# Constant matmuls on TensorE at five stage borders of a fused two-layer transformer kernel

## The chip, the cores and the metric

The kernel runs on one NeuronCore of one Trainium2 chip. The metric is the device time of one launch in microseconds (us). Five engines work side by side and meet through semaphores: TensorE (PE; its weight loads are listed apart as PEld), VectorE (DVE), ScalarE (ACT), GpSimd (POOL) and SyncE (SP), which here only issues DMAs. TensorE has two clock levels, 1.2 and 2.4 GHz; the profile gives the granted share of the higher one (0.50 or 1.00, or a mean between them over a stretch).

## The reference, cut to what matters

Two transformer layers on x of 4 x 1024 tokens x 128 channels, all in f32:

```python
x = x + attn0(layernorm(x))    # 16 heads of 8 channels, relative position bias with a gate
x = x + ffn0(layernorm(x))     # 16 experts of 64, grouped top-k routing, one shared expert
x = x + attn1(layernorm(x))    # 8 heads, q and k of 64 channels, values of 128, summed over heads
x = x + ffn1(layernorm(x))     # FP4-quantised linear layers, 352 hidden channels
```

The routing sorts per token: `scores = sigmoid(x @ w_gate.T)`, the two best of four groups by the sum of their two best scores, and of their experts the four best, whose scores are divided by their sum.

## The kernel before, in words

The program is a list of stages, each a block of its own: weights, `phase_project0`, `phase_attend0`, `phase_output0`, `phase_route`, `phase_experts`, `phase_project1`, `phase_attend1`, `phase_quant_ffn`. At the end of each block every engine drains its own work and meets the others at a barrier (the rows of L434, L1169, L1290, L1415, L1577 in the trace); so the engine that finishes last, SP's waits for stores included, sets when the next block begins. Within a block each engine has its own instruction stream, in the order in which the code is written, and TensorE runs its matmuls strictly in that order.

`phase_project0` works on 8 chunks of 512 tokens: layer norm, transposes, q, k, v and gates; its last act is that SP stores q and k to DRAM and waits until they have landed. `phase_attend0` has 64 items (16 heads x 4 batches) of 8 tiles of 128 queries. Row maxima are computed `LEAD` = 12 tiles ahead of the exponentials: TensorE writes a score tile of 128x1024 into two of three ring banks (L853 the far part, L867 the diagonal band), DVE reduces each 128x512 half to its maximum (L1048), and the bank is free again. So the stage opens with 12 tiles of maxima alone (the lead), then comes for each tile the score product for the exponential (L889, L899), ACT's exp (L1032) and the product with the values (L947). After 8 tiles the maxima of the first item are turned on TensorE (L964), go by ACT and SP into the operand of the exp product, and the first exp product waits for that DMA.

`phase_output0` is a software pipeline over the 8 chunks, written by `pipeline(eng, stages)`: at step s a stage with lag k works on chunk s - k, and the stages are issued in the order of the list. On TensorE that is the output projection (L1227, lag 2), the transpose of the normalised x (L1234, lag 4), the transpose of the attention output (L1220, lag 1) and the routing product (L1241, lag 5). DVE adds the bias (L1253), adds to x (L1256), takes the statistics and normalises (L364); POOL copies the attention output (L1177) and takes the reciprocal root; ACT moves transposed data out of PSUM.

`phase_route` ranks the experts on DVE alone. TensorE waits for the result (`ready`), turns it in 8 groups of four 128x128 transposes (L1368), and ACT copies each group out (L1375).

`phase_project1` makes q and k of the second attention (three f16 products L382 to L384 for each output of 128x512) and again ends when its stores have landed. `phase_attend1` has 32 items and the same lead of 12 tiles of maxima: two matmuls of 512 columns per tile (L1826), each reduced by DVE (L1949). In the steady state it is two matmuls per exp product (L1836, L1837) and three per value product (L1848 to L1850).

Before its first matmul in a block TensorE runs `credit` (L63), semaphore increments that come one after the other.

Of the kernel before, what the change touches and what calls it, by code (L numbers as in the profile page):

```python
# [368 lines left out]
def steps(eng, body, total=NC):  # L369


    with eng.Fori(0, total // 2 - 1) as i:
        body(2 * i, 0, False)
        body(2 * i + 1, 1, False)
    body(total - 2, 0, False)
    body(total - 1, 1, True)


def product16(nc, out, w, x):


    nc.tensor.matmul(out, w[:, 0, :], x[0], start=True, stop=False)  # L382
    nc.tensor.matmul(out, w[:, 0, :], x[1], start=False, stop=False)
    return nc.tensor.matmul(out, w[:, 1, :], x[0], start=False, stop=True)  # L384
# [7 lines left out]
def phase_project0(nc, g, a):  # L392
# [4 lines left out]
    with ExitStack() as ctx:  # L397
# [36 lines left out]
        with nc.Block() as block:  # L434
# [67 lines left out]
            def _(pe):  # L502
# [31 lines left out]
                    nc.tensor.matmul(ps[:, GR, 0:CT * H0], g.flip[:, :], gate[:, u, :, :], start=True, stop=True).then_inc(s.gate_turned, 1)  # L534

                steps(pe, step)

            @block.vector
            def _(dve):
# [110 lines left out]
def phase_attend0(nc, g, a):  # L650
# [9 lines left out]
    with ExitStack() as ctx:  # L660
# [22 lines left out]
        EXP, RING, AV = 0, 4, 7  # L683
# [55 lines left out]
        with nc.Block() as block:  # L739
# [87 lines left out]
            def _(pe):  # L827
# [132 lines left out]
                def turn_m(h, b, at):  # L960
# [3 lines left out]
                    nc.tensor.matmul(ps[0:2 * TB, RING + at % BANKS, 0:P], mm[:, b % 2, :, :, :].rearrange("p x y t -> p (x y t)"), ident16[:, :],  # L964
                                     start=True, stop=True).then_inc(s.m_turned, 1)

                for t in range(LEAD):
                    if t % TB == 0:
                        wait_loaded(0, t // TB)
                    at = [lead.index((t, half)) for half in range(2)]  # L970
                    for x in at:
                        if x >= BANKS:
                            if lead[x - BANKS] == "m":
                                pe.wait_ge(s.m_moved, done(0))
                            else:
                                pe.wait_ge(s.max_read, done(2 * lead[x - BANKS][0] + lead[x - BANKS][1]))
                    maxima(t // TB, t % TB, [RING + (x + shift) % BANKS for x in at])
                    if t == TB - 1:
                        at = lead.index("m")
                        pe.wait_ge(s.max_read, done(2 * lead[at - BANKS][0] + lead[at - BANKS][1]))  # L980
                        turn_m(0, 0, FIRST_M)
# [135 lines left out]
def pipeline(eng, stages, total=NC):  # L1117

    lag = max(k for k, _ in stages)
    pairs = (total - lag) // 2

    def straight(s):
        for k, stage in stages:
            if 0 <= s - k < total:
                stage(s - k, (s - k) % 2)

    for s in range(lag):
        straight(s)  # L1130
    with eng.Fori(0, pairs) as i:
        for r in range(lag, lag + 2):
            for k, stage in stages:
                stage(2 * i + (r - k), (r - k) % 2)
    for s in range(lag + 2 * pairs, total + lag):
        straight(s)


def phase_output0(nc, g, a):

    with ExitStack() as ctx:
# [27 lines left out]
        with nc.Block() as block:  # L1169
# [43 lines left out]
            def _(pe):  # L1213
# [27 lines left out]
                        last = nc.tensor.matmul(ps[:, R, k * NE:(k + 1) * NE], xTs[:, u, k * P:(k + 1) * P], g.routeW[:, :], start=True, stop=True)  # L1241
                    last.then_inc(s.r_psum, 1)

                pipeline(pe, [(2, project), (4, turn_x), (1, turn_a), (5, route)])

            @block.vector
            def _(dve):
# [19 lines left out]
def phase_route(nc, g, a):  # L1267


    with ExitStack() as ctx:  # L1270
# [19 lines left out]
        with nc.Block() as block:  # L1290
# [71 lines left out]

            @block.tensor
            def _(pe):
                pe.wait_ge(ready, 1)
                for c in range(NC):
                    for k in range(CT):
                        ins = nc.tensor.transpose(ps[0:2 * NE, c, k * P:(k + 1) * P], parts[:, c * CT + k, :], g.ident[:, :])  # L1368
                    ins.then_inc(turned, 1)
# [177 lines left out]
def phase_project1(nc, g, a):  # L1547

    with ExitStack() as ctx:
# [27 lines left out]
        with nc.Block() as block:  # L1577
# [56 lines left out]
            def _(pe):  # L1634
# [23 lines left out]
                        product16(nc, ps[:, QK + i % RING, :], g.w16[:, :, IN_16[W_Q1 + i], :], x).then_inc(s.qk_psum, 1)  # L1658

                pipeline(pe, [(2, lambda n, u: project(n, u, FIRST)), (1, turn_x), (2, lambda n, u: project(n, u, REST))])  # L1660

            @block.vector
            def _(dve):
# [25 lines left out]
def phase_attend1(nc, g, a):  # L1689
# [5 lines left out]
    with ExitStack() as ctx:  # L1695
# [19 lines left out]
        EXP, MAX, AV, OUT = 0, 2, 4, 6  # L1715
# [37 lines left out]
        with nc.Block() as block:  # L1753
# [57 lines left out]
            def _(pe):  # L1811
# [40 lines left out]
                def project_y(h, b, k, last_item=False):  # L1852
# [14 lines left out]
                        last = nc.tensor.matmul(out, y[0], w[1], start=False, stop=True)  # L1867
                    last.then_inc(s.out_psum[k], 1)

                for t in range(LEAD):  # L1870
                    score_max(0, t // TB, t % TB)
                    if t == TB - 1:
                        turn_m(0, 0)
# [404 lines left out]
```

## Time and profile before

| | us |
|---|---|
| median of 3 runs (lowest, highest) | 2301.78 (2299.64, 2307.66) |
| the profiled execution | 2315.67 |
| its span, first to last instruction | 2313.9 |
| TensorE busy | 2010.6 (87%) |
| VectorE busy | 1630.1 (70%) |
| ScalarE busy | 1347.9 (58%) |
| GpSimd busy | 1091.8 (47%) |
| mean granted TensorE clock | 0.943 |

The profiled execution took 13.9 us more than the median of the runs, and 1.8 us of its time lie outside of the span. Times in the trace count from the span's start. TensorE's busy time contains the latency at the end of each matmul, so the distance between the starts of two matmuls that follow each other closely, not the duration of one, is what a matmul costs.

### The profile page before, as it was taken

How to read it: one execution, taken by the hardware profiler on the slowest of the kernel's cores; microseconds unless marked ns; L12 is line 12 of the kernel's file. 1: busy time of each engine (PE TensorE's matmuls, PEld its weight loads, DVE VectorE, ACT ScalarE, POOL GpSimd, SP SyncE). 2: the span in 40 equal slices, each digit the busy share in tenths (PEclk: the TensorE clock that was granted, in tenths of full speed). 3: DMA queues.
4: the chain of work that ended last, by engine and by line, in shares of the span. 5: the costliest groups of instructions: out<-in, count | busy, mean ns of one | idle time of the engine just before them, and what ended most of it. 6: DMA issues, size and time to landing. Idle time of an engine off the chain costs nothing. (4 is left out here: it accounts for less than half of the span.)

```text
span 2313.9 us, 56417 instructions
## 1 busy us (share of the span) xinstructions
PE 2010.6 (87%) x17787; PEld 1018.8 (44%) x17787; DVE 1630.1 (70%) x3441; ACT 1347.9 (58%) x2150; POOL 1091.8 (47%) x939
## 2 busy tenths in 40 slices
PE   5569999999999989875799759999999999997666
PEld 3324444444444444434344214444444444443444
DVE  4778888888888877767666776666666666664696
ACT  2226666666666655552455437777777777776221
POOL 1132322322232222324355317777877787777454
PEclk9869999999999999986899979999999999999797
DMA  5522211221122121100000460011111011100000
GB/s 132 154 62 53 55 51 48 55 54 49 51 55 51 48 55 46 48 11 1 1 1 0 144 201 29 29 42 28 41 28 42 28 42 28 42 14 1 0 19 19
DMA packets 127068, 107.33 MB, mean 46 GB/s; under 512 B 39636, under 2 KB 102724, under 8 KB 126956
## 3 DMA queue, kind: packets, MB, share of 16 engines
q1 hardware_dynamic: 124640, 103.37, 16.3%
q10 hardware_dynamic: 2316, 2.64, 0.4%
q8 instruction: 49, 0.80, 0.1%
q14 instruction: 63, 0.52, 0.1%
HBM read 76.01 MB, written 29.53 MB: 46 GB/s over the span
## 5 line engine op out<-in xcount | busy, mean ns | idle before, releaser
L1048 DVE TENSOR_REDUCE b_mx<-psum 128x1 f32<-128x512 f32 x1024 | 663.5, 686 | 160.2 <-PE psum L867 92.9
L1032 ACT ACTIVATE b_prob<-psum 128x1024 f32<-128x1024 f32 x512 | 523.9, 1023 | 334.1 <-PE psum L899 334.0
L1806 POOL TENSOR_TENSOR f_plo<-f_prob,f_phi 128x512 f16<-128x512 f32 x512 | 586.8, 1156 | 170.2 <-ACT f_phi L1931 145.2
L1949 DVE TENSOR_REDUCE f_mx<-psum 128x1 f32<-128x512 f32 x512 | 328.4, 682 | 169.5 <-PE psum L1826 168.4
L1930 ACT ACTIVATE f_prob<-psum 128x512 f32<-128x512 f32 x512 | 308.1, 602 | 158.3 <-PE psum L1837 153.5
L947 PE MATMUL psum<-b_prob,b_v 128*32 128x256 f32 x4096 | 330.3, 394 | 1.6 <-ACT b_prob L1032 0.5
L1931 ACT ACTIVATE f_phi<-psum 128x512 f16<-128x512 f32 x512 | 306.9, 599 | 0.0
L805 POOL COPY b_v<-v 128x64 f32 x64 | 15.1, 236 | 610.2 <-PE psum L947 609.8
L899 PE MATMUL psum<-b_diag,b_toep 128*128 128x79 f16 (+1 forms) x4224 | 269.2, 209 | 0.0
L899 PEld LDWEIGHTS psum<-b_diag,b_toep 128*128 128x128 f16 x4224 | 237.5, 99 | 9.4 <-issue 2.6
L808 POOL TENSOR_TENSOR b_diag<-flip,grev 128x1024 f16<-128x1024 f16 x128 | 239.6, 1892 | 0.0
L1836 PE MATMUL psum<-f_qa,f_ka 128*128 128x512 f16 x512 | 195.2, 381 | 10.4 <-ACT f_phi L1931 7.2
L1848 PE MATMUL psum<-f_phi,v 128*128 128x512 f16 x512 | 194.3, 380 | 1.0 <-DVE f_yT L1968 0.5
L1837 PE MATMUL psum<-f_qb,f_kb 128*128 128x512 f16 x512 | 194.8, 380 | 0.0
L1849 PE MATMUL psum<-f_phi,v 128*128 128x512 f16 x512 | 194.0, 379 | 0.0
L1850 PE MATMUL psum<-f_plo,v 128*128 128x512 f16 x512 | 194.0, 379 | 0.0
L1826 PE MATMUL psum<-f_ka,f_qa 128*128 128x512 f16 x512 | 165.4, 392 | 19.0 <-DMA f_kb<-d_qk 13.2
L867 PE MATMUL psum<-b_toep,b_diag 128*128 128x286 f16 (+2 forms) x640 | 150.4, 269 | 0.0
L1512 POOL TENSOR_TENSOR d_h<-d_hid,d_h 128x512 f16<-128x512 f32 x72 | 83.2, 1157 | 110.8 <-ACT d_h L1482 110.8
L1968 DVE SCALAR_TENSOR_TENSOR f_yT<-psum,f_yT 128x512 f16<-128x512 f32 x64 | 44.2, 691 | 94.6 <-ACT f_yT L1917 94.6
L867 PEld LDWEIGHTS psum<-b_toep,b_diag 128*128 128x128 f16 x640 | 51.4, 97 | 115.3 <-issue 115.3
L947 PEld LDWEIGHTS psum<-b_prob,b_v 128*32 128x32 f32 x4096 | 81.2, 108 | 44.3 <-ACT b_prob L1032 1.0
(312 smaller groups left out, 3407.9 us busy)
## 6 DMA issues: line engine op xcount, KB each, us to landing
d_qk<-e_qk SPq DMA_DIRECT2D x64, 256.0 KB, 2.6
b_toep<-d_line SPq DMA_DIRECT2D x128, 64.0 KB
f_qa<-d_qk SPq DMA_DIRECT2D x64, 128.0 KB, 2.8
f_ka<-d_qk SPq DMA_DIRECT2D x64, 128.0 KB, 2.9
b_q<-d_q SPq DMA_DIRECT2D x128, 54.0 KB
d_k<-a_qk SPq DMA_DIRECT2D x48, 128.0 KB, 2.3
b_toep<-d_line SPq DMA_DIRECT2D x128, 32.0 KB
b_q<-b_m SPq DMA_DIRECT2D x256, 1.0 KB
```

What stands on the lines that cost most here:

```text
L808: ins = nc.gpsimd.tensor_tensor(diag[:, b, part, :, :], g.flip16[:, :].rearrange("p (a n) -> p a n", a=1).to_broadcast([P, TB, P]), gates. ...
L867: return nc.tensor.matmul(ps[:, bank, n0 - c0:n1 - c0], diag[:, b, 0, t, :], toep[:, b, 0, u:u + n1 - n0], start=False, stop=True, skip_gr ...
L899: last = nc.tensor.matmul(ps[:, bank, at + x:at + y], toep[:, b, tp, blk * P:(blk + 1) * P], diag[:, b, dp, qt, x:y], start=False, stop=(t ...
L947: last = nc.tensor.matmul(ps[32 * c:32 * c + VW, AV, 0:2 * P], vs[:, b, t, :], prob[:, t % 4, c * 2 * P:(c + 1) * 2 * P], start=t == 0, st ...
L1032: nc.scalar.activation(prob[:, t % 4, :].rearrange("p (a n) -> p a n", a=2), ps[:, EXP + 2 * (t % 2):EXP + 2 * (t % 2) + 2, :], ACT.Exp).t ...
L1048: nc.vector.tensor_reduce(mx[:, b, t, half:half + 1], ps[:, bank, :], AX.X, ALU.max).then_inc(s.max_read, 1)
L1806: nc.gpsimd.tensor_tensor(plo[:, t % 4, at], prob[:, t % 4, at], phi[:, t % 4, at], ALU.subtract).then_inc(s.plo_ready, 1)
L1836: nc.tensor.matmul(ps[:, EXP + half, :], ka[b][:, keys], qa[b][:, queries], start=True, stop=False)
L1837: nc.tensor.matmul(ps[:, EXP + half, :], kb[b][:, keys], qb[b][:, queries], start=False, stop=True).then_inc(s.exp_psum, 1)
L1930: nc.scalar.activation(prob[:, t % 4, at], ps[:, EXP + half, :], ACT.Exp)
L1931: nc.scalar.activation(phi[:, t % 4, at], ps[:, EXP + half, :], ACT.Exp).then_inc(s.exp_ready, 1)
L1949: nc.vector.tensor_reduce(mx[:, b, t, half:half + 1], ps[:, MAX + half, :], AX.X, ALU.max).then_inc(s.max_read, 1)
```

## The change

A helper `keep_busy` issues `count` matmuls of a constant f16 128x128 (`flip16`) with a constant f16 128x512 (`expert`) into a PSUM bank whose content nobody reads any more or yet. Nothing waits for them and they wait for nothing, but they stand in TensorE's stream, which is in order, and in its drain at the end of a block. The numbers are 48 at the end of `phase_project0` and 48 at the start of `phase_attend0`, 20 at the start of `phase_output0` and 6 at the end of each of 8 of its steps, 110 at the start of `phase_route`, 40 at the end of `phase_project1` and 40 at the start of `phase_attend1`. These are the whole diff.

```diff
+def keep_busy(nc, g, bank, count):
+
+    for _ in range(count):
+        nc.tensor.matmul(g.ps[:, bank, :], g.flip16[:, :], g.expert[:, 0:4, :].rearrange("p f e -> p (f e)"), start=True, stop=True)
...
                 steps(pe, step)
+                keep_busy(nc, g, 1, 48)
...
+                keep_busy(nc, g, AV, 48)
                 for t in range(LEAD):
                     if t % TB == 0:
                         wait_loaded(0, t // TB)
...
-                pipeline(pe, [(2, project), (4, turn_x), (1, turn_a), (5, route)])
+                keep_busy(nc, g, 7, 20)
+                pipeline(pe, [(2, project), (4, turn_x), (1, turn_a), (5, route), (1, lambda n, u: keep_busy(nc, g, 7, 6))])
...
             def _(pe):
+                keep_busy(nc, g, 0, 110)
                 pe.wait_ge(ready, 1)
                 for c in range(NC):
...
                 pipeline(pe, [(2, lambda n, u: project(n, u, FIRST)), (1, turn_x), (2, lambda n, u: project(n, u, REST))])
+                keep_busy(nc, g, 6, 40)
...
+                keep_busy(nc, g, AV, 40)
                 for t in range(LEAD):
                     score_max(0, t // TB, t % TB)
```

TensorE's stream at the start of `phase_output0` before: the transpose of the attention output (`c_at`), the output projection (`c_aT`), the transpose of the normalised x (`c_xn`). The line numbers after the change are higher by 8 here.

```order
L1212 UNCONDITIONAL_BRANCH
L1220 MATMUL psum<-square,c_at 128x128 x4
L1227 MATMUL psum<-wT,c_aT 128x128 x4
L1220 MATMUL psum<-square,c_at 128x128 x4
L1227 MATMUL psum<-wT,c_aT 128x128 x4
L1220 MATMUL psum<-square,c_at 128x128 x4
L1227 MATMUL psum<-wT,c_aT 128x128 x4
L1234 MATMUL psum<-square,c_xn 128x128 x4
```

And the same place now, with the constant matmuls as `expert,flip`:

```order
L1220 UNCONDITIONAL_BRANCH
L382 MATMUL psum<-expert,flip 128x512 x20
L1228 MATMUL psum<-square,c_at 128x128 x4
L382 MATMUL psum<-expert,flip 128x512 x6
L1235 MATMUL psum<-wT,c_aT 128x128 x4
L1228 MATMUL psum<-square,c_at 128x128 x4
L382 MATMUL psum<-expert,flip 128x512 x6
L1235 MATMUL psum<-wT,c_aT 128x128 x4
L1228 MATMUL psum<-square,c_at 128x128 x4
```

The 20 stand ahead of the first real work of the stage, and the 6 stand between the last product of a step and the projection that opens the next one.

TensorE's stream from the end of `phase_project1` (f16 products of `x` and `w`) into `phase_attend1` (score products of `f_ka` and `f_qa` for the maxima), now:

```order
L390 MATMUL psum<-x,w 128x512
L382 MATMUL psum<-expert,flip 128x512 x40
L1587 UNCONDITIONAL_BRANCH
L1821 UNCONDITIONAL_BRANCH
L382 MATMUL psum<-expert,flip 128x512 x40
L1837 MATMUL psum<-f_ka,f_qa 128x512 x16
L1829 MATMUL psum<-square,f_negm 8x128
```

Before, the two branches with the barrier between them followed the last product directly, and the first score product followed the branches. From `phase_project0` into `phase_attend0` it is the same with 48 and 48.

## Rows read from the trace of the kernel before

**Rows 1.** The page, busy tenths in 40 slices: TensorE's granted clock

```profile
PEclk9869999999999999986899979999999999999797
```

**Rows 2.** Windows: busy us of PE, PEld, DVE, ACT, POOL, granted clock, DMA share, GB/s

```profile
100.00:105.00 5.00, 0.00 (x0) 0.00 (x0) 3.94 (x9) 0.00 (x0) 0.00 (x0) 0.68 0.70 202
...
125.00:130.00 5.00, 2.82 (x12) 0.69 (x12) 2.80 (x5) 0.00 (x0) 5.00 (x5) 0.50 0.38 104
...
150.00:155.00 5.00, 5.00 (x62) 2.52 (x59) 2.97 (x6) 2.38 (x3) 0.00 (x0) 0.70 0.00 0
...
1070.00:1075.00 5.00, 3.09 (x25) 2.78 (x25) 4.84 (x21) 1.85 (x5) 2.94 (x4) 0.96 0.01 3
...
1115.00:1120.00 5.00, 4.89 (x27) 3.35 (x25) 0.00 (x0) 3.60 (x8) 0.00 (x0) 0.60 0.00 0
```

**Rows 3.** Timeline (start, us, engine, line, idle before), f16 matmuls early in phase_experts

```profile
1121.87 0.38 PE L384 MATMUL psum<-x,w 128*128 128x512 f16 x1
...
1122.09 0.38 PE L382 MATMUL psum<-x,w 128*128 128x512 f16 x1
```

**Rows 4.** Timeline, end of phase_project1 and start of phase_attend1

```profile
1355.44 0.63 PE L383 MATMUL psum<-x,w 128*128 128x512 f16 x1
...
1355.86 0.63 PE L384 MATMUL psum<-x,w 128*128 128x512 f16 x1
...
1360.11 0.38 PE L384 MATMUL psum<-x,w 128*128 128x512 f16 x1
...
1373.67 1.03 PE L1826 MATMUL psum<-f_ka,f_qa 128*128 128x512 f16 x2 [13.18 <-DMA f_kb<-d_qk]
...
1374.32 11.04 DVE L1949 TENSOR_REDUCE f_mx<-psum 128x1 f32<-128x512 f32 x16 [4.64 <-PE psum L1826]
```

**Rows 5.** TensorE's credits after the barriers of three blocks: count, ns, first and last

```profile
L63 PEldq EVENT_SEMAPHORE  x7: 51/51/51, 1366.6 to 1367.6; - x7
...
L63 PEldq EVENT_SEMAPHORE  x6: 51/51/51, 114.1 to 114.9; - x6
...
L63 PEldq EVENT_SEMAPHORE  x4: 51/51/51, 1037.8 to 1038.2; - x4
```

**Rows 6.** Timeline, end of phase_project0 and first tiles of phase_attend0

```profile
97.40 0.33 PE L534 MATMUL psum<-a_gate,square 128*128 128x64 f32 x2
...
125.26 0.28 PE L853 MATMUL psum<-b_k0l,b_q 32*128 32x128 f16 x1 [27.53 <-DMA b_toep<-d_line]
...
129.78 1.29 DVE L1048 TENSOR_REDUCE b_mx<-psum 128x1 f32<-128x512 f32 x2 [0.55 <-PE psum L867]
...
146.61 0.61 PE L889 MATMUL psum<-b_q,b_k0l 32*128 32x512 f16 x2 [0.20 <-DMA b_q<-b_m]
...
153.19 1.02 ACT L1032 ACTIVATE b_prob<-psum 128x1024 f32<-128x1024 f32 x1 [1.57 <-PE psum L899]
...
154.67 1.02 ACT L1032 ACTIVATE b_prob<-psum 128x1024 f32<-128x1024 f32 x1 [0.46 <-PE psum L899]
```

**Rows 7.** Timeline, phase_output0

```profile
1038.69 1.12 PE L1220 MATMUL psum<-square,c_at 128*128 128x128 f32 x4 [9.57 <-POOL c_at L1177]
...
1042.59 0.69 DVE L1253 TENSOR_TENSOR c_o<-psum,bvo 128x512 f32<-128x512 f32 x1 [5.18 <-PE psum L1227]
...
1051.27 0.69 DVE L1253 TENSOR_TENSOR c_o<-psum,bvo 128x512 f32<-128x512 f32 x1 [1.93 <-PE psum L1227]
...
1068.16 0.66 PE L1234 MATMUL psum<-square,c_xn 128*128 128x128 f32 x4 [0.35 <-DVE c_xn L364]
...
1070.47 1.16 PE L1227 MATMUL psum<-wT,c_aT 128*128 128x128 f32 x8
...
1071.83 0.68 DVE L1253 TENSOR_TENSOR c_o<-psum,bvo 128x512 f32<-128x512 f32 x1
```

**Rows 8.** Timeline, phase_route

```profile
1113.65 6.24 PE L1368 MATMUL psum<-square,r_parts 128*32 128x128 f32 x32 [29.96 <-DVE r_parts L1355]
...
1114.73 0.57 ACT L1375 CAST combT<-psum 32x512 f16<-32x512 f32 x1 [30.78 <-PE psum L1368]
```

## The prediction

> **What bounds the kernel now.** I read first the line of the granted clock over the whole span [rows 1]. The reader is to see that it is at 2.4 GHz (9, in tenths) almost everywhere: the dips lie at slices 2 and 3, 18 to 20 and 24, and near the end. All that a warmer TensorE could give lies there. Then I went through the dips in stretches of 5 us [rows 2], and through the timeline at each border [rows 4, 6 to 8], asking two questions: what does TensorE wait for there, and is it TensorE at all that sets the pace once it works?
>
> The answer differs from place to place. In the gap between the projection and the first attention (97.7 to 125.3) TensorE waits for DMAs: the first product comes after 27.53 us idle, released by a load [rows 6]. In the 12 tiles of maxima that follow, a DVE pair of 1.29 us sets most of the pace, and DVE waits 0.55 us for a slow product in the tile shown [rows 6]. In the output projection DVE is busy 4.84 of 5 us [rows 2]. In the routing TensorE waits 29.96 us for DVE's ranks, and then turns 32 tiles in 6.24 us at the low clock [rows 8]. Before the second attention it waits 13.18 us for stores, barrier and loads, and then DVE's 16 reductions take 11.04 us, 0.69 each, with nothing between them [rows 4]: that stretch cannot get faster by the clock.
>
> **The price of one constant matmul.** Products of the same form, an f16 weight of 128x128 and 512 columns, start 0.22 us apart at 2.4 GHz (1121.87 and 1122.09) [rows 3], and 0.42 us apart at 1.2 GHz (1355.44 and 1355.86) [rows 4]. From 512 columns I take 0.215 and 0.427. So n of them cost 0.215 n, plus half of the time that passes before the clock rises. How long is that? In the routing the turns began at 1113.65 and the slice 1115 to 1120 has a mean clock of 0.60, so it rose at about 1119.0: 5.3 us [rows 2, 8]. In the first attention close work began at 146.61, and a mean of 0.70 in 150 to 155 puts the rise at 153.0: 6.4 us [rows 2, 6]. I take 5.3, which adds 2.6 us, and as bounds 2.7 us (half of it, no row shows less) and 6.4 us, which add 1.3 and 3.2.
>
> **Start of the first attention.** The 48 at the end of the projection begin at 97.7 at full clock, end at 108.1 and are over before SP's stores let the barrier pass near 114: nothing. But the clock does not survive what follows. After the last work at 97.73 it fell within 100 to 105 (mean 0.68, so at 101.8) [rows 2, 6], 4.1 us later, and from 108.1 to the next constants there are 6.8 us. These wait for TensorE's own credits, of which the last is at 114.9 [rows 5]. They end at 114.95 + 48 x 0.215 + 2.6 = 127.9, and the first real product waited only until 125.26: **2.6 us later** (1.3 to 3.3). What is queued behind is the whole lead, and DVE waits for it. In return the first two or three tiles of the lead run at 2.4 GHz and save DVE some 0.4 each of its 0.55, say 1.0. The first exp product waited 0.20 us for the DMA of the maxima at 146.61, which now is there: another 0.3 with the issue before it. Sum **+1.3**. I do not count on the clock holding through the lead: there TensorE was busy 2.82 of 5 us at the low clock, about half of that at the high one, and in 1070 to 1075 the clock fell with 3.09 of 5 us busy [rows 2].
>
> **The output projection.** TensorE's credits end at 1038.25 [rows 5], and the first turn stood ready at 1038.69 [rows 7]. The 20 constants begin with the clock low and end at 1038.25 + 4.3 + 2.6 = 1045.2: **+6.5** (5.2 to 7.1). Nothing covers that: POOL's copy is done, and ACT, DVE and the rest of the chain start from this turn. At the high clock the way from the first turn to DVE's first sum (1038.69 to 1042.59, 3.90 us) becomes 0.43 + 6 constants of 1.29 + a projection of 1.16, about 3.0, and from there to the third sum (1051.27) it loses some 0.7 as well: -1.6 [rows 7]. Then each step holds 6 constants. From a turn of x at 1068.16 to the end of the next projection (1070.47 + 1.16) it was 3.47 us; with 1.29 more it is 4.76. DVE's own step is about 3.8 us: 3.67 from this turn, which DVE's last instruction released, to its next sum at 1071.83, and the time to wake. The turn waits for DVE's step, and DVE's step after the next waits for that projection, so two steps take 4.76 + 0.05 + 3.8 = 8.6, or 4.3 each. The five steps from 1051.27 to 1071.83 took 4.11 each, the cold ones included, so the five lose 0.95. The tail has no constants between its turns and stays as it is. Sum 6.5 - 1.6 + 0.95 = **+5.9**. So the constants inside the loop about pay for themselves, the 20 ahead of it do not.
>
> **The routing.** The 110 take 23.7 + 2.6 = 26.3 us of the gap of 29.96, and nothing waits for them. They end about 3.2 us before the ranks are ready. If the clock holds, the 8 groups are paced by ACT's 0.57 instead of 0.78 (6.24 / 8): 8 x 0.21 = 1.7 us less [rows 8]. A pause of 3.2 us is near the 4.1 us above, so I count half: **-0.8** (0 to -1.7).
>
> **The second projection and attention.** The last product starts at 1360.11 and the constants at 1360.33 [rows 4]; 40 x 0.215 = 8.6 puts TensorE's drain at about 1369.1. The barrier was open at 1366.55, as the first credit at 1366.6 shows [rows 5]: everything in the next block, SP's loads too, is **2.8 us** later. The credits, which took until 1367.65, then end at 1370.45. The clock is still up. 40 more end at 1379.1, and the first score product was at 1373.67; its load now lands at 1376.5 and no longer decides. The lead starts **5.45 us** later in all, the 2.8 included. DVE's pace there is its own [rows 4], so a high clock returns 0.3, at the first wait and at the turn of the maxima: **+5.1**. Once the exp products begin the stage is bound by TensorE for 700 us, so no slack takes this back.
>
> **Sum.** 1.3 + 5.9 - 0.8 + 5.1 = 11.5 us. The profiled execution, 2315.67, would become 2327; it was 13.9 above the median of the runs, for which the forecast is 2301.78 + 11.5 = **2313.3 us**. About 0.3% (6.9 us) is what a measurement of this kernel can tell from no change.
>
> **One rule against the rows.** Rows 3 say 0.215 us for a constant. The Trainium skill, in TensorE: Matmul & The Clock Gate, section Back-to-back issue gap, gives for a sustained stream of weight loads and matmuls of 512 columns about 131 ns each. This case's trace disagrees, with its 0.22 us between two such starts [rows 3]. By the page 40 constants would take 5.2 us instead of 8.6, the sum of the second attention would be near nothing, and the whole change, by an estimate from that page, near +4 us.
>
> **The rivals.**
> 1. *The constants are cheaper than rows 3 say, because they need nobody's result* (0.06). The point at which it decides is the second projection: at or under 0.15 us each, 40 fit into the 6 us between 1360.33 and the barrier and into the 6.0 us between credits and load, and the 5.1 goes. For it speaks nothing in the rows but that products of 32 rows start together in other places; against it [rows 3]. Time: 11.5 - 5.1 - 1.3 - 1 = +4, 2306. The page's figure above would have this outcome.
> 2. *The clock holds through both leads into the exp products* (0.17), which is the way to "not slower". Its place is 128 to 150. Then DVE loses its waits in all tiles of the lead (another 1.5 us), and the first exps come 1.1 us earlier each (idle 1.57 at 153.19, 0.46 at 154.67) [rows 6], some 2.0 in all; the routing gives its full 1.7, and the second attention's first exps 0.6. That is -3.5 - 0.9 - 0.6: **+6.5**, 2308.3. It decides when the granted clock is 1.00 from 128 to 153. Against it stands the fall at 3.09 of 5 us busy.
> 3. *Constants do not raise the clock* (0.05), since they are mostly zeros. Then 48, 20, 110 and 40 cost 0.427 each: 20.5 us against 10.3 at the first attention, 8.5 ahead of the output projection and 2.6 in each of its steps (some 20 us), 47 against 30 in the routing, 17 against 6 twice: about +70, 2372.
> 4. *The stages do not start from TensorE's stream as I read it, or steady stages settle in another rhythm* (0.07), either sign, 2295 to 2325.
>
> The forecast itself has 0.65.
>
> **How the numbers follow.** Within the likeliest case the bounds of the clock's rise (-2.6 to +1.2 over both places), the routing (-0.9 to +0.8) and the repeat of a median of 2301.78 (some 3 us) give 2308 to 2319. Reaching to rivals 1 and 2 on one side, and on the other to a clock that rises late and to an experts stage that begins cold, makes 2303 to 2322, which leaves out rival 3 and most of 4. Slower by over 0.3% means above 2308.7: nearly all of the forecast, less than half of rival 2, rival 3, part of 4, together 0.68. Faster than 2294.9 is left to rival 4 and to what I overlook: 0.08. The rest, 0.24, is the same.
>
> **What would show each step.** In the profile of the changed kernel: constants 0.215 us apart, at 0.427 for 2.7 to 6.4 us after each cold start; the first product of the first attention at 126.6 to 128.6, released by TensorE's own stream and no longer by a DMA; clock 0.50 again before 140; the first turn of the output projection some 6.5 us after the credits, and steps of 4.3 us; the ranks ready after the constants end; the drain of the second projection ending last on TensorE, and the first score product 9.8 us after its barrier and not 7.1. The prediction would be wrong if the lead of the first attention ran at 1.00 throughout and its tiles came 0.3 us apart closer, if the constants stood closer than 0.2 us, or if the 20 turned out to begin before the barrier.

## The result, and the profile after

The changed kernel took 2313.33 us (median; 2309.67 to 2317.40), beside 2301.22 us for the kernel before on the same chip: a ratio of 1.0046, 95% interval 1.003 to 1.0062. It is slower by 12 us by this comparison, and the fastest single runs lie 10 us apart too (2309.67 and 2299.64). The profiled execution took 2314.96 us, its span is 2313.2 us and its mean clock 0.959. That is no longer than the profiled execution of before (2315.67 us), and this section and the next show why both numbers hold.

The clock over the 40 slices, as in [rows 1]:

```profile
PEclk8979999999999999988999999999999999999797
```

The dips at slices 20 and 24 are gone, slice 19 rises from 6 to 8, and slices 2 and 3 rise by one tenth each (8 and 6 before, 9 and 7 now). The windows show where the clock came up and where it did not stay (columns as in [rows 2]):

```profile
125.00:130.00 5.00, 4.32 (x22) 1.74 (x20) 0.65 (x2) 0.00 (x0) 5.00 (x5) 1.00 0.39 106
130.00:135.00 5.00, 2.55 (x12) 0.71 (x12) 3.85 (x8) 0.00 (x0) 1.67 (x1) 0.64 0.45 121
...
150.00:155.00 5.00, 5.00 (x43) 2.35 (x43) 3.08 (x6) 2.05 (x2) 0.00 (x0) 0.50 0.01 3
...
1110.00:1115.00 5.00, 4.41 (x25) 3.29 (x26) 0.54 (x1) 2.64 (x5) 0.00 (x0) 0.66 0.00 0
```

In 125 to 130 the clock is at its high level where it was at 0.50; in 130 to 135 it falls, after two tiles of the lead, and at 150 it is as low as it ever was. Now the start of the first attention, to be laid beside [rows 6] (start, us, engine, line, idle before):

```profile
97.00 10.52 PE L382 MATMUL psum<-expert,flip 128*128 128x512 f16 x48
115.46 13.34 PE L382 MATMUL psum<-expert,flip 128*128 128x512 f16 x48 [7.93 <-PEq L440]
128.73 0.23 PE L860 MATMUL psum<-b_k0l,b_q 32*128 32x128 f16 x1
...
151.46 1.02 ACT L1040 ACTIVATE b_prob<-psum 128x1024 f32<-128x1024 f32 x1 [7.15 <-PE psum L906]
```

The same 48 matmuls take 10.52 us warm and 13.34 us when the clock starts low, and the first real product comes behind them with no DMA named. The first exp starts at 151.46. In the kernel before it was this row, with a barrier 0.45 us earlier:

```profile
148.73 1.02 ACT L1032 ACTIVATE b_prob<-psum 128x1024 f32<-128x1024 f32 x1 [7.25 <-PE psum L899]
```

The output projection, beside [rows 7]:

```profile
1027.41 7.00 PE L382 MATMUL psum<-expert,flip 128*128 128x512 f16 x20 [9.22 <-PEq L746]
...
1034.25 0.60 PE L1228 MATMUL psum<-square,c_at 128*128 128x128 f32 x4
...
1037.31 1.46 PE L382 MATMUL psum<-expert,flip 128*128 128x512 f16 x6
...
1041.80 0.66 PE L1228 MATMUL psum<-square,c_at 128*128 128x128 f32 x4 [2.14 <-POOL c_at L1185]
1042.29 2.26 PE L382 MATMUL psum<-expert,flip 128*128 128x512 f16 x6
...
1044.34 1.92 PE L1235 MATMUL psum<-wT,c_aT 128*128 128x128 f32 x8
...
1046.30 0.69 DVE L1262 TENSOR_TENSOR c_o<-psum,bvo 128x512 f32<-128x512 f32 x1 [2.53 <-PE psum L1235]
...
1064.00 0.69 DVE L1262 TENSOR_TENSOR c_o<-psum,bvo 128x512 f32<-128x512 f32 x1 [0.87 <-PE psum L1235]
...
1067.98 0.68 DVE L1262 TENSOR_TENSOR c_o<-psum,bvo 128x512 f32<-128x512 f32 x1
```

The first turn waits for the 20. Each later group of 6 takes 1.46 us, but the one after TensorE's wait for POOL (2.14 us) takes 2.26, and the projection behind it 1.92 instead of 1.16: the clock fell just behind that wait. DVE's last two sums are 3.98 us apart, the two before them 4.77: it waits for TensorE in every second step.

The second projection and attention, beside [rows 4]; the first row is one of the barrier's (duration three times, first and last start):

```profile
L1587 PEldq DRAIN  x1: 4050/4050/4050, 1362.3 to 1362.3; - x1
...
1367.69 8.79 PE L382 MATMUL psum<-expert,flip 128*128 128x512 f16 x40 [1.36 <-issue]
1376.32 0.59 PE L1837 MATMUL psum<-f_ka,f_qa 128*128 128x512 f16 x2
...
1376.73 10.45 DVE L1961 TENSOR_REDUCE f_mx<-psum 128x1 f32<-128x512 f32 x16 [7.03 <-PE psum L1837]
```

TensorE's drain ends at 1366.35 and releases the barrier at 1366.5, where SP was ready at 1363.8. The first score product comes 9.8 us after it. DVE's 16 reductions take 10.45 us instead of 11.04.

**Length of each block.** The whole time of this kernel scatters by several us for a reason shown below, so the experiments are read by blocks. A block's length is the time from TensorE's release at one barrier to that at the next, as in these rows of the changed kernel, 1026.5 - 114.4 = 912.1 us for the first attention (such rows are rounded to 0.1 us, and so are the lengths):

```profile
L440 PEldq EVENT_SEMAPHORE  x1: 51/51/51, 114.4 to 114.4; - x1
...
L746 PEldq EVENT_SEMAPHORE  x1: 51/51/51, 1026.5 to 1026.5; - x1
```

| block | without constants (profiles) | changed kernel, profiled twice | difference |
|---|---|---|---|
| first projection | 76.95 (6: 76.9 to 77.0) | 77.9, 78.4 | +1.2 |
| first attention | 909.0 (2 free of stalls), 914.8 to 923.6 (6 others) | 912.1, 911.8 | +2.9 against 909.0 |
| output projection | 46.4 (10: 45.4 to 48.1) | 54.5, 53.7 | +7.7 |
| routing | 36.5 (9: 35.8 to 36.9) | 35.9, 34.3 | -1.4 |
| experts | 163.9 | 163.8, 163.9 | 0 |
| second projection | 82.3 (10: 81.2 to 83.4) | 85.8, 85.1 | +3.2 |
| second attention | 766.9 (10: 766.3 to 767.4) | 767.6, 769.3 | +1.6 |

The sum is +15.2 us. Two blocks are not in the table, since no constants stand in them: the weights (35.1 to 37.5 us) and the last one, `phase_quant_ffn` (178.7 to 181.1 us). They differ by over 2 us from profile to profile with their instructions unchanged. In the first pair of profiles the last block alone gives the changed kernel 2.1 us.

The kernel before pays part of that in another way: its first attention in the profile is 923.6 us long, since it holds two stalls (engine, line, idle before):

```profile
867.29 0.61 PE L889 MATMUL psum<-b_q,b_k1l 32*128 32x512 f16 x2 [3.74 <-issue]
...
869.13 1.02 ACT L1032 ACTIVATE b_prob<-psum 128x1024 f32<-128x1024 f32 x1 [5.10 <-PE psum L899]
...
928.37 0.61 PE L889 MATMUL psum<-b_q,b_k1l 32*128 32x512 f16 x2 [4.57 <-issue]
```

"issue" means that TensorE waited for nothing that the profile shows. Both places are the first work behind the back edge of the attention's loop (the jump back to its first instruction), 61.1 us apart, which is one pass. The changed kernel has no such wait.

### The profile page after: what moved, and what is told of

Same layout as the page of the kernel before. It is cut to its first block and busy times, and to the rows that moved or that the text cites. A ratio compares the mean times of both kernels' runs of the same rounds, so it can differ in the third digit from the quotient of the medians.

```text
span 2313.2 us, 57125 instructions
## 1 busy us (share of the span) xinstructions
PE 2075.1 (90%) x18141; PEld 1045.6 (45%) x18141; DVE 1632.1 (71%) x3441; ACT 1347.0 (58%) x2150; POOL 1091.4 (47%) x939
## 5 line engine op out<-in xcount | busy, mean ns | idle before, releaser
L1056 DVE TENSOR_REDUCE b_mx<-psum 128x1 f32<-128x512 f32 x1024 | 663.9, 686 | 148.5 <-PE psum L874 85.1
L382 PE MATMUL psum<-expert,flip 128*128 128x512 f16 x354 | 86.1, 404 | 19.1 <-PEq L746 9.2
```

What stands on the lines that cost most here:

```text
L1056: nc.vector.tensor_reduce(mx[:, b, t, half:half + 1], ps[:, bank, :], AX.X, ALU.max).then_inc(s.max_read, 1)
```

## The experiments

### One place at a time

The first four kernels each keep the constants of one place. The second attention:

```diff
+                keep_busy(nc, g, 6, 40)    # end of phase_project1
+                keep_busy(nc, g, AV, 40)   # start of phase_attend1
```

> Only the 40 constants at the end of the second projection and the 40 at the start of the second attention. My theory (a constant costs 0.215 us in TensorE's in-order stream, and what it exceeds its gap by is lost): barrier 2.8 us later, first score product 9.8 us after the barrier and not 7.1, +5.1 us in all, ratio 1.0022. Rival (the loss of the whole change comes from other places, such as instruction fetch or the output projection): within 1 us of before, and the first score product still released by its load.

Measured: second projection 85.2 us, second attention 767.9, first score product 9.78 us after its barrier: the same as in the changed kernel. The whole: 2315.19 us, ratio 1.003 (0.9996 to 1.0064). These two blocks cost +2.9 and +1.0 by this profile. The lead starts 2.4 us later than without constants (7.2 to 7.5 us after the barrier), but the sixth exp only 1.0 later (32.9 us after the barrier against 31.5 to 32.1): the warm clock returns over 1 us in the lead.

The 20 ahead of the output projection:

```diff
+                keep_busy(nc, g, 7, 20)
```

> Only the 20 constants ahead of the output projection. My theory: its first turn comes 7.4 to 8 us after the barrier and not 1.1, +6.5 us, of which the steps return less than 1 since without the six per step the clock falls again: block of 52 us and not 46.5, ratio 1.0025. Rival (a warm start pays the wait back): block of 47 to 49 us.

Measured: block 50.1 us, +3.7 against 46.4; whole 2304.81 us, ratio 0.9997 (0.9973 to 1.0021). The first turn is 7.9 us behind the barrier instead of 1.1; from it to DVE's third sum it takes 10.34 us instead of 12.6, and from the third to the eighth 19.45. Without constants that last stretch takes 19.5 us in five of ten profiles, where the clock holds, and 20.6 to 22.1 in the others, where it falls once more on the way. So the 20 give back 2.2 us in the fill, and 1.0 in the loop against the mean of 20.5, and pay 6.8 for it. The block lies between the two readings, 52 and 47 to 49.

The two places around the first attention:

```diff
+                keep_busy(nc, g, 1, 48)    # end of phase_project0
+                keep_busy(nc, g, AV, 48)   # start of phase_attend0
```

> Only the 48 at the end of the first projection and the 48 at the start of the first attention. My theory: first product some 3 us later than before, the clock falls again within the lead, sum +1.3 us (0 to 2.5), ratio 1.0006. Rival (the clock at the start is worth its wait): -2 us or less.

Measured: first projection 78.4 us, first attention 911.7 and no stall, first exp 36.8 us after the barrier; whole 2304.03 us, ratio 0.9973 (0.9951 to 0.9995).

The 110 ahead of the routing's turns:

```diff
+                keep_busy(nc, g, 0, 110)
```

> Only the 110 constants in the routing. My theory: they cover 26 of 30 us and then the clock falls or holds by chance, routing block 34.9 to 36.6 us and not 36.6, -0.8 us on average, ratio 0.9997. Rival (the clock surely holds): -1.7 us, block of 34.9 with a granted clock of 1.00 through the turns.

Measured: routing 35.8 us; whole 2307.83 us, ratio 1.0012 (0.9986 to 1.0038). The clock did not hold through the turns, though the constants end only 2.70 us before them (the window 1105 to 1110 has 0.73):

```profile
1107.06 5.34 PE L1375 MATMUL psum<-square,r_parts 128*32 128x128 f32 x32 [2.70 <-DVE r_parts L1361]
```

Two kernels without the 110 had 35.8 and 35.9 us (the one above, and the one with the 6 per step below), so a single profile doesn't decide this term.

The kernel with the first attention's constants should have been 1 to 3 us slower than before and came out faster. Its block had no stall, those of the other three had 1, 2 and 1. So the question became whether this is chance.

### The kernel before again, and the 6 per step alone

> The kernel before, unchanged, to see how much of a difference its own executions make. In the four experiments so far the first attention without any constants was 914.8, 916.7, 922.7 and (kernel before) 923.6 us long, and held 1, 1, 2 and 2 stalls of TensorE of 4 to 5 us just behind its loop's back edge. If these stalls are chance in each execution, this one may hold any number from 0 to 2. If they belong to the program's code as placed, it holds 2 again and the block is near 923 us. Either way the other blocks should repeat within 1 us: projection 77, output projection 45 to 48, routing 36.5, second projection 82 to 83, second attention 767. Ratio 1.000.

Measured: 2306.64 us, ratio to itself 1.0028 (1.0001 to 1.0055); first attention 915.8 us with one stall; all other blocks within 1.2 us of the first profile. So two groups of runs of one and the same kernel differ by 0.3%, with an interval that leaves out 1: here a ratio within 0.3% of 1 says little by itself. And the number of stalls changes from one execution of the same kernel to the next.

```diff
-                pipeline(pe, [(2, project), (4, turn_x), (1, turn_a), (5, route)])
+                pipeline(pe, [(2, project), (4, turn_x), (1, turn_a), (5, route), (1, lambda n, u: keep_busy(nc, g, 7, 6))])
```

> Only the 6 constants at the end of each step of the output projection. Against four blocks without constants there (45.4, 46.6, 48.1, 48.1 us, mean 47.05) the prediction's step says about nothing: the steady steps grow from 4.11 to 4.3 us, and the fill gives 1.6 us back. The blocks with the 20 alone (50.1) and with both (54.5) say instead that the 6 per step cost 4.4 us. If they do so by themselves, this block is 50 to 52 us long and its steps alternate between 3.9 and 4.8 us; if it was only the pair, or a pause that happened to let the clock fall in the changed kernel, it is 46 to 48. The rest as in the kernel before; the whole time +0 to +4 us, which the timed runs can hardly tell.

Measured: block 48.0 us, below the 50 to 52 of one reading and at the upper edge of the other, +1.6 against the mean of 46.4, which is within the scatter of 45.4 to 48.1; whole 2308.48 us, ratio 1.0019 (0.9995 to 1.0042). Its timeline shows the alternation:

```profile
1061.65 1.05 PE L1233 MATMUL psum<-wT,c_aT 128*128 128x128 f32 x8
...
1062.74 0.69 DVE L1259 TENSOR_TENSOR c_o<-psum,bvo 128x512 f32<-128x512 f32 x1 [0.87 <-PE psum L1233]
...
1066.71 0.68 DVE L1259 TENSOR_TENSOR c_o<-psum,bvo 128x512 f32<-128x512 f32 x1
```

From the third sum to the eighth it takes 21.70 us, in the changed kernel 21.68 and 21.70. The 20 alone cost 3.7 and the 6 alone 1.6, both together 7.7, which is 2.4 more than the sum. With the 6 behind them the 20 no longer bring the short loop (21.7 us instead of 19.45), because now TensorE and no longer DVE sets every second step; and of the 2.2 us in the fill 0.6 are left.

### Counts cut to the gaps

```diff
+                keep_busy(nc, g, 1, 48)    # end of phase_project0, as in the change
+                keep_busy(nc, g, AV, 36)   # start of phase_attend0, was 48
+                keep_busy(nc, g, 0, 122)   # phase_route, was 110; none in phase_output0
+                keep_busy(nc, g, 6, 26)    # end of phase_project1, was 40
+                keep_busy(nc, g, AV, 27)   # start of phase_attend1, was 40
```

> The same constants cut to what the waits of the profile can hold: 48 at the end of the first projection, 36 ahead of the first attention, none in the output projection, 122 ahead of the routing's turns, 26 at the end of the second projection, 27 ahead of the second attention. If a constant matmul costs only its own 0.215 us in TensorE's stream (theory), then: first product of the first attention as early as in the kernel before plus at most 0.3 us, the lead a little faster; output projection 47; routing 35.5; barrier after the second projection as before (82.5); first maximum product of the second attention 7.2 to 7.4 us after its barrier as before and the block 766.5. Sum -1 to -2.5 us against blocks free of stalls, and with the stalls of the first attention gone as in the changed kernel, 2300 to 2303 us in all, ratio 0.996 to 0.999. Rival: constants cost something beyond their time in the stream (the drain, the barrier, a colder start of what follows), then the second projection and attention stay 1 us or more longer although nothing waits for TensorE, and the whole is at or above the kernel before.

Measured: first attention 908.3 us, output projection 48.1, routing 34.3, second projection 83.2, second attention 766.4; whole 2300.59 us, ratio 0.9979 (0.996 to 0.9998). The 27 still put the first score product at 8.4 us after the barrier instead of 7.3, but the sixth exp comes at 31.4 us, no later than without constants. The rival's extra cost beyond the time in the stream is not to be seen: 83.2 is within the scatter of 81.2 to 83.4.

### What the constants do to the place of the code

```diff
+                keep_busy(nc, g, 1, 48)    # end of phase_project0, alone
```

> Only the 48 at the end of the first projection, which lie in the wait for its stores: 77 to 78 us for that block by both theories. What it is for is the first attention, whose instructions are unchanged but lie 48 matmuls further on in TensorE's code. In the profiles so far that block held 2 stalls of 4 to 5 us behind the loop's back edge in two kernels without constants ahead of it, 1 in two others, and 0 in both kernels with constants ahead of it (911.7 and 912.1 us, 2.4 of them from the late start). Theory one, placement: moving the code is enough, the stalls are gone, the block takes 909 to 911 us, and the timed runs lie within 5 us of each other as those of the two kernels without stalls did. Theory two, the warm clock or the constants at the start of the attention remove them: here the clock has fallen again before the attention starts, so the block holds 1 or 2 stalls, 914 to 923 us. Theory three, chance: any number.

Measured: first attention 909.0 us, no stall; 2299.14 us, all runs within 7.4 us of each other, ratio 0.9979 (0.9965 to 0.9993). The clock was low again when the attention began (0.50 from 115 to 150). So it is placement, or TensorE's work, but not the clock. The next kernel has no work:

```diff
+                for _ in range(96):
+                    pe.sem_inc(g.x_loaded, 1)
```

> No constant matmul at all: in the place of the 48 (each a weight load and a matmul) at the end of the first projection stand 96 increments of a semaphore that nobody waits for, some 5 us of TensorE's queue inside the wait for the stores, and the same number of instructions ahead of the first attention's loop. Theory one, placement: the stalls of 4 to 5 us behind the loop's back edge are gone, the first attention takes 909 to 910 us, the runs lie within 8 us of each other and the median is 2298 to 2300. Theory two, TensorE's work or clock: the block holds 1 or 2 stalls, 914 to 923 us, and the runs spread over 15 us or more. By theory one SP's late store in the first projection (1.2 to 1.8 us instead of 0.33, in all four kernels with the 48) tells more: if it is gone here (block 77.0), the matmuls' traffic caused it; if it stays (78.3), the code did.

Measured: first attention 909.0 us, no stall; 2300.27 us, ratio 0.9972 (0.9953 to 0.9992). The increments run in TensorE's queue from 96.5 to 111.2, inside the wait for stores. So 96 instructions without any matmul remove the stalls as 48 constants do. And with a third as many instructions:

```diff
+                keep_busy(nc, g, 1, 16)    # end of phase_project0, alone
```

> 16 constants instead of 48 at the end of the first projection, so that the loop of the first attention is moved by 32 instructions instead of 96. If any move removes the stalls: 0 stalls, 909 us. If what counts is where exactly the loop's instructions come to lie: 1 stall or 2 may be left, 914 to 918 us. If it is chance (the kernel before itself had 2 and 1): any number, and runs spread over 15 us or more.

Measured: **2406.73 us, ratio 1.0434 (1.0398 to 1.047)**. None of the expectations had that. All blocks but one are as ever; the first attention takes 1014.3 us, 105.3 more than 909.0, and holds 14 stalls, 61 us apart, one for each pass of the loop from the second on. One of them in its timeline, the load of the first score product behind the back edge:

```profile
217.44 0.10 PEld L896 LDWEIGHTS psum<-b_q,b_k1l 32*128 32x128 f16 x2 [3.35 <-issue]
...
218.76 1.02 ACT L1039 ACTIVATE b_prob<-psum 128x1024 f32<-128x1024 f32 x1 [3.69 <-PE psum L906]
...
220.63 0.19 PEld L954 LDWEIGHTS psum<-b_prob,b_v 128*32 128x32 f32 x5 [1.92 <-issue]
```

Two waits stand here with "issue", 3.35 and 1.92 us, and behind them the clock is low for a stretch (window of the same kernel):

```profile
220.00:225.00 5.00, 4.37 (x36) 1.66 (x37) 1.36 (x3) 1.40 (x2) 3.12 (x3) 0.50 0.29 43
```

The group of that weight load, in this kernel and then in the one with 96 increments (busy and mean ns, then idle before it in us):

```profile
L896 PEld LDWEIGHTS psum<-b_q,b_k1l 32*128 32x128 f16 x192 | 12.9, 96 | 50.3 <-issue 50.3
```

```profile
L897 PEld LDWEIGHTS psum<-b_q,b_k1l 32*128 32x128 f16 x192 | 12.3, 92 | 6.6 <-issue 6.6
```

The page's row of the queue that carries instructions points to what TensorE waits for. In the kernel before, with the 16 constants, with the 96 increments, and in the changed kernel:

```profile
q8 instruction: 49, 0.80, 0.1%
```

```profile
q8 instruction: 157, 2.57, 0.4%
```

```profile
q8 instruction: 32, 0.52, 0.1%
```

```profile
q8 instruction: 34, 0.56, 0.1%
```

The first two numbers are packets and MB. It is 8 to 9 packets of 16 KB more for each stall, over all profiles of the study:

| instructions ahead of the loop, more than before | kernels | stalls | q8 packets | first attention, us |
|---|---|---|---|---|
| 0 | before, before again, and the four with one other place | 2, 1, 1, 2, 1, 1 | 49, 40, 41, 49, 41, 41 | 914.8 to 923.6 |
| 32 | 16 constants | 14 | 157 | 1014.3 |
| 96 | 48 constants, 96 increments | 0, 0 | 32, 32 | 909.0, 909.0 |
| 168 | 48 and 36 constants (twice) | 0, 0 | 33, 33 | 908.3, 907.8 |
| 192 | changed kernel (twice), 48 and 48 constants | 0, 0, 0 | 34, 34, 32 | 911.7 to 912.1 |

The same row for stretches of the trace says when the packets come. In the kernel before there is none from 220 to 860, and 13 from 860 to 935, which holds the two stalls. With the 16 constants they come in each pass, 112 from 215 to 980; with the 96 increments there is none from 215 to 980.

```profile
q8 instruction: 13, 0.21, 1.4%
```

```profile
q8 instruction: 112, 1.84, 1.0%
```

In the four profiles with one stall, which lies between 213 and 225, 9 packets come from 213 to 290 and none from 290 to 970. So from the second pass on the loop fetches nothing in a pass without a stall, and a stall stands where some 9 packets are fetched again.

The two kernels with 96 show that the stalls go away when 96 instructions of either kind stand ahead of the loop. The 14 stalls with 32 more instructions were not repeated with 32 increments, so there the place of the code is argued, not shown. That the stalls are fetches of instructions is read from the packets, their times and the place behind the back edge; no run here took the fetch itself away. Which offsets are good could not be told from five of them.

### The free places together, and the changed kernel again

```diff
+                keep_busy(nc, g, 1, 48)    # end of phase_project0
+                keep_busy(nc, g, AV, 36)   # start of phase_attend0
+                keep_busy(nc, g, 0, 122)   # phase_route
```

> Only the constants that the block lengths so far show to be free or better: 48 at the end of the first projection, 36 ahead of the first attention, 122 ahead of the routing's turns; nothing in the output projection or around the second attention. Theory (each place by itself): first attention 908 to 909 us and without a stall as in the kernel with the cut counts (908.3), routing 34.3 against 36.5 to 36.9, output projection 45.4 to 48.1, second projection 81 to 83, second attention 766.5; against the kernel with the 48 of the projection's end alone (2299.1 us) that is 0.7 + 2.2 = 3 us less, 2296 us, ratio 0.996 to 0.998, the upper end if the output projection loses its clock once more. Rival: what the routing gives back is taken again by the blocks behind it, as the kernel with the cut counts hinted (2300.6 us although these two blocks gave 3 us); then it is 2299 to 2301.

Measured: first attention 907.8 us, output projection 45.4, routing 34.3; 2298.98 us, ratio 0.9967 (0.9946 to 0.9988). It beats both kernels, the changed one by 14 us. The kernel with 96 idle increments, timed with it, took 2300.27 us, so of the gain over the kernel before most is the placement; 1.3 us are left to the warm clock where the profile promised 3, and that is not more than the runs scatter. The routing in this kernel's timeline:

```profile
1066.68 28.72 PE L382 MATMUL psum<-expert,flip 128*128 128x512 f16 x122 [0.57 <-PEq L1177]
...
1096.12 3.67 PE L1377 MATMUL psum<-square,r_parts 128*32 128x128 f32 x32 [0.71 <-DVE r_parts L1363]
```

The constants end 0.71 us before the ranks, and the 32 turns take 3.67 us instead of 6.24 [rows 8].

> The changed kernel itself once more, on the same chip as the other three. Blocks as in its first profile: projection 78, first attention 912 and no stall, output projection 54.5 if TensorE's clock falls in the wait for the third chunk's copy as it did (52.5 if not), routing 36, second projection 85.5, second attention 767.7; 2313 us, and 13 to 15 us above the kernel with the 48 of the projection's end alone. If the two blocks of the output projection differ by over 1 us, the term that came out too large was chance in one profile.

Measured: 2313.39 us, ratio 1.0027 (0.9999 to 1.0054) against a kernel before that took 2305.91 us this time. The changed kernel repeats to 0.1 us; it is the kernel before that moves, from 2302 to 2307 us in three groups of runs on this chip, with 2301 beside the first result and 2308 on the chip of the first four experiments. So by this second comparison of whole times alone the change could not be told from no change. Output projection 53.7 us with the same fall of the clock, so its term was no chance. The routing took 34.3 us this time, and 35.9 in the first profile. The turns in the first profile, after 110 constants, and then here:

```profile
1110.59 5.34 PE L1378 MATMUL psum<-square,r_parts 128*32 128x128 f32 x32 [4.28 <-DVE r_parts L1364]
```

```profile
1110.04 3.67 PE L1378 MATMUL psum<-square,r_parts 128*32 128x128 f32 x32 [3.79 <-DVE r_parts L1364]
```

In the first profile the clock fell right behind the wait of 4.28 us (0.66 in the window of 1110 to 1115 above), here it held behind 3.79 us. But in the kernel with the 110 alone it fell behind 2.70 us, so the length of the wait alone doesn't decide it. The 110 brought the short turns in one profile of three, the 122, which leave less than 1 us, in both of two.

## Why the prediction was right, and where not

The time, 2313.3 forecast and 2313.33 measured, was right, and the likeliest case was the one that came. But two errors of several us cancelled in it, and the agreement to 0.1 us is luck. Step by step:

- **Price of a constant.** 0.215 us: confirmed, 48 in 10.52 us. The cold start added 2.6 in the forecast; the 48 of the first attention took 13.34 us, so it added about 2.8 here. The rule of the Trainium skill (TensorE: Matmul & The Clock Gate, Back-to-back issue gap) that the prediction weighed, 131 ns, does not hold for this stream.
- **First projection, forecast 0.** Mis-sized: +1.2. TensorE's drain was over long before SP, as said, but one of SP's stores is issued late. In the kernel with the 48 alone it is this row, 1.66 us where the same store took 0.33 in the kernel before:

```profile
98.69 1.66 SPq L457 DMA_DIRECT2D d_q<-a_g  x1
```

  It is so in 5 of the 6 profiles with 48 constants there (1.2 to 1.8 us), and not in those with 16 or with increments; the block with the 96 increments took 77.6 all the same. What holds the store is open.
- **Start of the first attention, forecast +2.6 - 1.3.** Right in kind: the first product came behind the constants (at 128.73, 0.1 later than the latest time named), and the clock was at 0.50 again before 140. By the first exp, 37.0 us after the barrier against 34.4, it is +2.5, and +2.9 by the block. The first product came 3.1 us later than without constants, where 2.6 were forecast. The return of the lead was mis-sized: 1.3 were forecast and some 0.6 came, since the clock fell after two tiles.
- **Output projection, forecast +5.9, measured +7.7.** The start: +6.5 forecast, +6.6 measured. The steady steps: five of 4.3 forecast (21.5 us), 21.7 measured, alternating as said (3.98 + 4.77 = 8.75 for two, 8.6 forecast). They cost 1.1 to 1.2 against 0.95. Mis-sized is the fill: -1.6 forecast, and from the first turn to the third sum it is 12.0 us instead of 12.6, -0.6. The first sum did come 1.1 us sooner after the turn (0.9 forecast); from the first to the third it took 0.4 to 0.5 us longer, where 0.7 less was forecast. The 18 constants between the first turn and the third projection cost 1.7 (10.34 us in the kernel with the 20 alone), the fall of the clock behind TensorE's wait for POOL among them. The prediction costed the fill as if the high clock were sure after the 20. The remaining 0.3 are in the tail, 13.02 and 12.35 us against 12.3, and not explained.
- **Routing, forecast -0.8 as the mean of 0 and -1.7.** Measured -0.6 and -2.2: it is the two-sided case that was forecast, with a larger gain. The -0.6 is not the constants' doing for sure, since two kernels without them had the same length. The prediction let the length of the pause decide (3.2 us beside 4.1); the clock fell behind 2.70 us and held behind 3.79, so more than that decides.
- **Second projection, forecast +2.8.** +3.2, with TensorE's drain ending last, as said.
- **Second attention, forecast +2.3 behind its barrier.** The start at 9.8 us was exact. The return was mis-sized: 0.3 forecast, and against a start 2.4 us later the block grew by only 0.7 and 2.4 us in the two profiles and by 1.0 in the kernel with this place alone, so 0 to 1.7 came back. Part of it is that DVE's 16 reductions shrank from 11.04 to 10.45 us, a stretch of which the prediction said that it cannot get faster by the clock.
- **What the prediction left out.** The sum of the terms by blocks is +15.2 against 11.5, and the timed runs agree: from the kernel with the 48 of the projection's end alone, 2299.14 us, to the changed one it is 14.2, and 1.2 of that block are in both. The constants ahead of the first attention also move its code, and with it went the stalls that cost the kernel before 6 to 15 us in each of six profiles, and some 1 to 9 us in its timed medians (2301 to 2308 us, against 2299.14 and 2300.27 in the two kernels that only moved the code). The profile showed them: two waits of 5.10 and 5.93 us of ACT for TensorE, "issue" in front. The prediction read the stage as steady and did not ask what 192 instructions ahead of a loop do to it. Of its rivals the fourth came nearest (a steady stage in another rhythm) but named no mechanism. Rival 1 is refuted by the first row of constants (48 in 10.52 us, 0.22 each), rival 2 by the window of 130 to 135, and rival 3 by the second row: 13.34 us, where 48 at the low clock would take 20.5.

## What to carry to other kernels

A matmul that nobody reads is free only inside a wait that it does not outlast, and the clock that it buys can be gone after the next short wait of the real work (2.14 us in the output projection). Here it paid in the routing, where the constants could be cut to end 0.7 us before the result, and elsewhere by 1.3 us at most (the first attention). Before judging any change by less than a per cent, count the "issue" waits behind the back edge of each long loop and the packets of the instruction queue, in both kernels: a change that adds instructions ahead of a loop can move the time by more than what it was made for. Compare the kernel before with itself as well, to see what ratio comes of no change at all. Read such a change by the length of its blocks, and time it beside a kernel that adds as many idle instructions.

## What the runs showed of the hardware that was not expected

- 32 more instructions ahead of TensorE's loop of 61 us per pass cost 105 us (14 stalls, 7.5 us each with the low clock behind it); with 96, 168 or 192 the 1 or 2 stalls that the loop had in each profile were gone. The instruction queue moved some 9 packets of 16 KB around each stall and, from the second pass on, none in a pass without one.
- The clock fell behind a wait of 2.14 us in the output projection and behind waits of 2.70 and 4.28 us in the routing, and held through one of 3.79 us in the routing.
- With 48 constants at the end of the first projection one DMA issue of SP took 1.2 to 1.8 us instead of 0.33 in 5 of 6 profiles.
